# Single products for the attention's running maxima, a fourth bank for the scores, and context products in blocks of four key tiles

## The chip, the core and the metric

The kernel runs on one core of a Trainium2 chip. The metric is the time of one execution on the device in microseconds (us), taken as the median of several runs. All activations are float32. The kernel is written engine by engine: TensorE (matrix products), VectorE, ScalarE and GpSimd each have a program of their own, in a fixed order, and wait for one another on semaphores. TensorE writes its results to PSUM, which has eight banks of 512 float32 columns on 128 partitions.

## What is computed

A layer of latent attention, a mixture of experts, a second causal attention and a second mixture of experts, on x of 16 batches by 100 tokens by 256. The change touches only the first attention, which is, for each batch b:

```python
x = x + attention(layernorm(x), ctx_512)
# in attention, 16 heads, 1444 keys, latent width 64:
scores = einsum('bhsr,bhlr->bhsl', q_r, k_r)     # 16 x 100 queries against 1444 keys
attn   = softmax(scores, axis=-1)
ctx_c  = einsum('bhsl,bld->bhsd', attn, kv_r)    # context: 64 wide
out    = (ctx_c through w_kc_kv, heads joined) @ Wo.T
```

## The kernel before

`latent_attention` (L393) works batch by batch. The queries of a batch are 1600 columns (16 heads of 100), held as a high and a low part in `QS` (128 rows: 64 high, 64 low) and `QB`; the rotated keys lie in `KH` and `KB`, again with high and low parts. The 1444 keys are 12 tiles of 128, and the 16 heads are done in two passes p of 8 heads, so a batch has 24 tiles n, and a step m is two of them (n = 2m and 2m + 1).

For a tile, `scores` (L805) makes two half tiles (o = 0, 1) of 128 keys by 400 query columns, two matmuls each, into one of three banks (`SB`, `S0`). ScalarE takes the exponential of each half tile (L780) into `R`, a ring of eight tiles (`EB`). VectorE adds the even halves in a bank (`sum_even`, L599) and GpSimd the odd halves (`sum_odd`, L615); these are the softmax's divisors. `values` (L817) multiplies the exponentials with the rotated keys into the context (two half tiles, each on 64 columns of the array, beside each other).

The softmax subtracts each query's maximum, and it is found one batch ahead. Queries times keys, by the high parts, give 39 pieces (`NF`): 13 tiles of 128 queries by three overlapping ranges of 482 keys. `max_pair` (L555) makes two pieces at once on the two halves of the array's rows (64 rows each, the high parts of queries and keys) into two banks (`F0`), and `reduce_pair` (L585) on VectorE takes both maxima with one instruction over 964 columns. The next pair waits until that is done. After the twentieth, `batch_max` joins the three ranges, `turn_max` (L571) turns the result on TensorE, `max_high` and `max_low` split it, and two transfers of SyncE put it into rows of `QB`, where the scores' second matmul adds it.

In a step of TensorE (L828 on) stand: a pair of maxima of the next batch (for m below 10), the scores of two tiles, another pair, and the context products of the two tiles before. At step 2 come the column sums of the batch before (`sums`, second pass), at step 8 those of the first pass; at step 9 the output projection of the batch before (`project`, L662), at step 10 the turn. These share the bank `MISC`. VectorE's loop over n (L900) has the reduction of pair n, the running sum of tile n - 1, and at fixed n other work: the reciprocal of the divisors (`RECIP_AT`, n = 9), the division of the context (`CT_AT`, n = 14), two parts of the keys' low rows for the batch after next (`LO_AT`, n = 18 and 20, `rotate_part`, L540), the addition of the output (`add_output`) and `max_low`. GpSimd rotates the keys of the batch after next between its sums.

Of the kernel before, what the change touches and what calls it, by code (L numbers as in the profile page):

```python
# [12 lines left out]
ALU = mybir.AluOpType  # L13
# [7 lines left out]
P = 128  # L21
# [371 lines left out]
def latent_attention(core, dram, X, ident, queries, recips, BB):  # L393
# [14 lines left out]
    SB, FB = 3, 2  # L408
# [3 lines left out]
    S0, F0, CTX, ACC, MISC = 0, 3, 5, 6, 7  # L412
    SUM_AT, SUM0_AT, OUT_AT, TURN_AT = 2, 8, 9, 10
# [5 lines left out]
    with ExitStack() as ctx:  # L419
# [128 lines left out]
        def f_bank(b, i):  # L548

            return S0 if b is FIRST and i % 2 else F0  # L550
# [4 lines left out]
        def max_pair(pe, b, i):  # L555

            r = b_mod(b)
            depth = 2 if b is FIRST else 1
            if i >= depth:
                pe.wait_ge(red_done, b_val(b) * NP + (i - depth + 1))  # L560
            elif b is not FIRST:
                pe.wait_ge(red_done, b_val(b) * NP)
            for f in pieces(i):
                t, j = divmod(f, KC)
                rows = slice((f % 2) * DC, (f % 2 + 1) * DC)
                high = QB if f % 2 else QS
                last = nc.tensor.matmul(psum[f_bank(b, i) + f % 2][:, 0:KW], high[r][rows, t * P:(t + 1) * P],  # L567
                                        KH[r][rows, KAT[j]:KAT[j] + KW], start=True, stop=True)
            last.then_inc(f_ready, 1)

        def turn_max(pe, b):  # L571
            pe.wait_ge(nm_ready, b_val(b) + 1)
            nc.tensor.transpose(psum[MISC][0:QT, 0:P], NM[:, :], ident[:, :]).then_inc(turned, 1)

        def max_high(act, b):
            act.wait_ge(turned, b_val(b) + 1)
            if b is not FIRST:
                act.wait_ge(m_in, b_val(b) * 32)
            nc.scalar.activation(MH[:, :], psum[MISC][0:QT, 0:P], ACT.Copy).then_inc(mh_ready, 1)

        def max_low(v, b):
            v.wait_ge(mh_ready, b_val(b) + 1)
            nc.vector.tensor_tensor(ML[:, :], psum[MISC][0:QT, 0:P], as_f32(MH[:, :]), ALU.subtract).then_inc(ml_ready, 1)

        def reduce_pair(v, b, i):  # L585
            v.wait_ge(f_ready, b_val(b) * NP + (i + 1))
            if i == 0 and b is not FIRST:
                v.wait_ge(nm_ready, b_val(b))
            k, n = f_bank(b, i), len(pieces(i))
            nc.vector.tensor_reduce(PM[:, 2 * i:2 * i + n], banks[:, k:k + n, 0:KW], AX.X, ALU.max).then_inc(red_done, 1)  # L590

        def batch_max(v, b):
            v.wait_ge(red_done, b_val(b) * NP + NP)
# [36 lines left out]
        def sums(pe, b, p):  # L630
# [5 lines left out]
            for o in range(2):  # L636
                last = nc.tensor.matmul(psum[MISC][o * DC:(o + 1) * DC, 0:CH], ones[:], ES[:, p, o, :], start=True, stop=True)
            last.then_inc(sum_done, 1)

        def sums_out(act, b, p):  # L640
# [3 lines left out]
            nc.scalar.activation(SU[:, p, :], psum[MISC][0:DC + 1, 0:CH], ACT.Copy).then_inc(su_done, 1)  # L644
# [17 lines left out]
        def project(pe, b):  # L662

            pe.wait_ge(ct_ready, b_val(b) + 2)
            for j in range(H // 2):
                last = nc.tensor.matmul(psum[MISC][0:S, 0:D], CT[:, j, :], BB[:, j, :], start=j == 0, stop=j == H // 2 - 1)
            last.then_inc(out_ready, 1)

        def add_output(v, b):
            v.wait_ge(out_ready, b_val(b) + 2)  # L670
            x = X[:, b_val(b), :]
            nc.vector.tensor_tensor(x, psum[MISC][0:S, 0:D], x, ALU.add).then_inc(res_done, 1)
# [28 lines left out]
        with nc.Block() as block:  # L701
# [50 lines left out]
            def _(act):  # L752
# [13 lines left out]
                def step(b, has_next, has_keys):  # L766
                    for n in range(NS):
                        if n == 2 * TURN_AT + 2 and has_next:
                            max_high(act, b + 1)
                        if n == 0 and b is not FIRST:  # L770
                            context_out(act, before(b), 1)
                        act.wait_ge(av_done, b_val(b) * NS + (n + 1))
# [10 lines left out]
                        if n == 2 * SUM_AT + 1 and b is not FIRST:  # L783
                            sums_out(act, before(b), 1)
                        if n == KT + 1:
                            context_out(act, b, 0)
                        if n == 2 * SUM0_AT + 1:
                            sums_out(act, b, 0)
# [6 lines left out]
            def _(pe):  # L795
# [5 lines left out]
                for i in range(NP):  # L801
                    max_pair(pe, FIRST, i)
# [25 lines left out]
                def step(b, has_next, has_keys):  # L828
                    for m in range(NS // 2):
# [3 lines left out]
                        if has_next and 2 * m < NP:  # L833
                            max_pair(pe, b + 1, 2 * m)
                        if m == 0:
                            if b is not FIRST:
                                for n in range(NS - 2, NS):
                                    values(before(b), n)
                            if has_next:
                                max_pair(pe, b + 1, 1)  # L840
                            pe.wait_ge(m_in, b_val(b) * 32 + 32)
                        for n in (2 * m, 2 * m + 1):
                            scores(b, n)
                        if has_next and m and 2 * m + 1 < NP:
                            max_pair(pe, b + 1, 2 * m + 1)
                        if m == TURN_AT and has_next:
                            pe.wait_ge(su_done, b_val(b) * 2 + 1)
                            if b is not FIRST:
                                pe.wait_ge(res_done, b_val(b))
                            turn_max(pe, b + 1)  # L850
# [3 lines left out]
                        if m == SUM_AT and b is not FIRST:  # L854
                            sums(pe, before(b), 1)
                        if m == SUM0_AT:
                            sums(pe, b, 0)
                        if m == OUT_AT and b is not FIRST:
                            pe.wait_ge(su_done, b_val(b) * 2 + 1)
# [1564 lines left out]
```

## Time and profile before

| | us |
|---|---|
| median of three runs | 1990.33 |
| lowest and highest of them | 1978.36, 1990.39 |
| the profiled execution | 1987.93 |
| its span, first to last instruction | 1986.1 |

The profile is of one execution, and its rows are durations of instructions on each engine. Several in a row may be joined in a line with a count (x8 instructions). A matmul in float32 counts as two instructions. TensorE's matmuls overlap, so what a matmul costs is read from the start of one to the start of the next, and not from its duration; the same holds, for the last 0.1 us, on VectorE. What stands in brackets is the time for which the engine stood idle before the instruction, and who ended it. PE is TensorE, PEld its weight load, DVE VectorE, ACT ScalarE, POOL GpSimd; L567 is line 567. The attention's loop over batches runs from about 335 to 1190 us.

### The profile page before, as it was taken

The numbers are of one execution on the slowest core, as the hardware profiler recorded it, in microseconds if no ns is written. First come the engines' busy times: TensorE is split into PE (matmuls) and PEld (weight loads), VectorE is DVE, ScalarE is ACT, GpSimd is POOL, SyncE is SP. The second block draws the span as 40 slices with busy tenths as digits, with TensorE's granted clock in tenths as the row PEclk, the third lists the DMA queues.
The fourth block names the chain that finished last, engine by engine and source line by source line (L and its number), as shares of the span: only waits on it lengthen the run. The fifth ranks groups of instructions, "written<-read, shape, count | busy, mean of one in ns | idle before, by whom it ended". The sixth has DMA issues, their size and how long they took to land. (4 is left out here: it accounts for less than half of the span.)

```text
span 1986.1 us, 29082 instructions
## 1 busy us (share of the span) xinstructions
PE 1710.8 (86%) x9602; PEld 1155.4 (58%) x9602; DVE 1313.9 (66%) x2408; ACT 769.1 (39%) x1996; POOL 902.8 (45%) x800
## 2 busy tenths in 40 slices
PE   4999935999999999999999996499999559987890
PEld 3677712555555555555555553399999547664780
DVE  5577768777777777777777744377767666666333
ACT  2100001444444444444444442266656237652230
POOL 0366623777777777777777440223322100000436
PEclk9999965999999999999999996599999879988795
DMA  6133344122122221122221002545555250001243
GB/s 183 39 72 71 67 125 150 39 72 61 45 72 72 72 64 56 63 72 72 72 72 35 10 9 54 152 163 201 183 173 196 85 130 0 0 1 37 89 122 102
DMA packets 91670, 166.50 MB, mean 84 GB/s; under 512 B 45635, under 2 KB 70439, under 8 KB 86735
## 3 DMA queue, kind: packets, MB, share of 16 engines
q1 hardware_dynamic: 83727, 145.77, 23.8%
q0 software_dynamic: 7808, 19.02, 3.8%
q8 instruction: 73, 1.20, 0.3%
q14 instruction: 62, 0.51, 0.1%
HBM read 134.91 MB, written 29.53 MB: 83 GB/s over the span
## 5 line engine op out<-in xcount | busy, mean ns | idle before, releaser
L780 ACT ACTIVATE R<-banks 128x400 f32<-128x400 f32 x768 | 333.7, 505 | 342.4 <-PE banks L814 340.0
L590 DVE TENSOR_REDUCE PM<-banks 128x2 f32<-128x964 f32 x320 | 360.8, 1132 | 155.8 <-PE banks L567 154.1
L628 POOL TENSOR_TENSOR EA<-EA,R 128x400 f32<-128x400 f32 x288 | 313.3, 1088 | 177.8 <-ACT R L780 164.6
L814 PE MATMUL banks<-QS,KH 128*128 128x400 f32 x768 | 309.5, 403 | 3.0 <-DMA QB<-ML 2.1
L824 PE MATMUL banks<-R,KV 128*64 128x400 f32 x1536 | 299.9, 512 | 0.0
L814 PE MATMUL banks<-QB,KB 128*128 128x400 f32 x768 | 266.2, 347 | 0.0
L608 DVE TENSOR_TENSOR banks<-banks,R 128x400 f32<-128x400 f32 x320 | 183.9, 575 | 54.9 <-ACT R L780 54.2
L814 PEld LDWEIGHTS banks<-QS,KH 128*128 128x128 f32 x768 | 145.2, 189 | 109.0 <-ACT R L780 58.5
L567 PE MATMUL banks<-KH,QS 64*128 64x482 f32 x320 | 160.5, 502 | 53.5 <-DVE KB L540 46.3
L175 PE MATMUL banks<-e_xh,e_split 128*116 128x256 f32 x960 | 195.7, 287 | 4.0 <-DVE e_xl L1586 4.0
L380 POOL TENSOR_TENSOR rotated<-rope_prod 96x400 f32<-96x400 f32 x128 | 131.7, 1049 | 131.7 <-DVE rope_prod L357 131.6
L567 PEld LDWEIGHTS banks<-KH,QS 64*128 64x128 f32 x320 | 60.9, 191 | 197.2 <-issue 111.6
L824 PEld LDWEIGHTS banks<-R,KV 128*64 128x64 f32 x1536 | 93.4, 136 | 120.0 <-ACT R L780 67.1
L357 DVE TENSOR_TENSOR rope_prod<-banks,rope_q 96x400 f32<-96x400 f32 x256 | 128.6, 561 | 51.0 <-PE banks L175 51.0
L175 PEld LDWEIGHTS banks<-e_xh,e_split 128*116 128x116 f32 x960 | 153.1, 183 | 4.4 <-DVE e_xl L1586 4.4
L567 PE MATMUL banks<-KH,QB 64*128 64x482 f32 x304 | 153.0, 504 | 0.0
L814 PEld LDWEIGHTS banks<-QB,KB 128*128 128x128 f32 x768 | 146.5, 191 | 0.4
L1461 POOL DMA_INDIRECT results<-e_ys,m_target x40 | 44.4, 1109 | 213.1 <-DVE e_ys L1604 207.0
L175 PE MATMUL banks<-e_xl,e_split 128*116 128x256 f32 x480 | 136.7, 285 | 0.0
L521 POOL TENSOR_TENSOR raw<-raw,ropeT 128x722 f32<-128x722 f32 x60 | 104.0, 1735 | 53.8 <-DMA rawk<-in_ctx_k 53.8
L1052 POOL IOTA m_steps<- 100x7 f32 (+1 forms) x2 | 0.3, 158 | 237.8 <-POOLq L70 237.8
L1611 DVE TENSOR_TENSOR e_HF<-banks,e_G 116x256 f32<-116x256 f32 x120 | 50.5, 421 | 86.9 <-ACT e_G L1550 85.9
(281 smaller groups left out, 3368.9 us busy)
## 6 DMA issues: line engine op xcount, KB each, us to landing
m_stage_u<-in_m_up SPq DMA_DIRECT2D x20, 1392.0 KB
raw<-in_ctx_T SPq DMA_DIRECT2D x16, 1444.0 KB, 6.2
m_stage_d<-in_m_down SPq DMA_DIRECT2D x20, 696.0 KB
QS<-queries SPq DMA_DIRECT2D x16, 800.0 KB, 6.8
queries<-q_out_h SPq DMA_DIRECT2D x64, 100.0 KB, 2.4
queries<-q_out_l SPq DMA_DIRECT2D x64, 100.0 KB, 2.4
QB<-queries SPq DMA_DIRECT2D x16, 400.0 KB, 8.1
RS<-recips SPq DMA_DIRECT2D x32, 200.0 KB
```

What stands on the lines that cost most here:

```text
L175: ins = nc.tensor.matmul(out, lhs, rhs, start=first and n == 0, stop=last and n == len(todo) - 1)
L357: last = nc.vector.tensor_tensor(prod[:, h % 2, n, :].rearrange("p (b s) -> p b s", b=CB), psum[2 * (h % 2) + half][0:HALF, 0:CH].rearrang ...
L380: last = nc.gpsimd.tensor_tensor(rot[:, h % TURNS, half, :], prod[:, h % 2, 2 * half, :], prod[:, h % 2, 2 * half + 1, :], ALU.add)
L521: ins = ops.tensor_tensor(raw[:, row, half], raw[:, row, half], ropeT[:, row, half], ALU.mult)
L567: last = nc.tensor.matmul(psum[f_bank(b, i) + f % 2][:, 0:KW], high[r][rows, t * P:(t + 1) * P], KH[r][rows, KAT[j]:KAT[j] + KW], start=Tr ...
L590: nc.vector.tensor_reduce(PM[:, 2 * i:2 * i + n], banks[:, k:k + n, 0:KW], AX.X, ALU.max).then_inc(red_done, 1)
L608: ins = nc.vector.tensor_tensor(acc, acc, tile_of(n, 0), ALU.add)
L628: nc.gpsimd.tensor_tensor(out, first, tile_of(n, 1), ALU.add).then_inc(odd_sum, 1)
L780: nc.scalar.activation(tile_of(n, o), psum[S0 + (2 * n + o) % SB][:, 0:CH], ACT.Exp).then_inc(exp_done, 1)
L814: last = nc.tensor.matmul(out, lhs[r][:, keys], heads[:, o], start=lhs is KH, stop=lhs is KB)
L824: last = nc.tensor.matmul(psum[CTX][o * DC:(o + 1) * DC, 0:CH], KV[b_mod(b)][:, t, :], tile_of(n, o), start=t == 0, stop=t == KT - 1)
L1611: nc.vector.tensor_tensor(HF[:, b, :], psum[b][0:TR, TOK:2 * TOK], G[:, b, :], ALU.mult).then_inc(h_ready, 1)
```

## The change

The scores get four banks instead of three. The maxima get two banks, 4 and 5, that also serve the turn, the sums and the projection, which have no bank of their own any more. A piece of the maxima is now one matmul of all 128 rows (the high and the low part of the queries against the keys' high part), written to the two banks in turn, and reduced by an instruction of its own (`max_row`, `reduce_row`). The piece f waits until the piece f - 2 is reduced. A step has four slots for such pieces: ahead of the scores (0), between the two tiles' scores (1), behind them (2), and at the end of the step (3); the table `MAX_AT` says which are used. The context products stand in every second step, for four tiles, between slots 2 and 3 (in step 0: between slot 0 and the scores). Projection and output addition come a step later, behind the turn. The first batch's maxima, ahead of the loop, use four banks in pairs.

```diff
@@ constants @@
-    SB, FB = 3, 2
+    SB = 4
...
-    S0, F0, CTX, ACC, MISC = 0, 3, 5, 6, 7
-    SUM_AT, SUM0_AT, OUT_AT, TURN_AT = 2, 8, 9, 10
+    S0, F0, CTX, ACC = 0, 4, 6, 7
+    SUM_AT, SUM0_AT, TURN_AT = 2, 8, 10
+    MAX_AT = ((1, 1, 1, 1),) * 3 + ((0, 1, 1, 1),) + ((1, 1, 1, 1),) * 4 + ((1, 1, 1, 0), (0, 1, 1, 1), (1, 1, 0, 0), (0, 0, 0, 0))
+    MAX_NO = [[sum(map(sum, MAX_AT[:m])) + sum(MAX_AT[m][:slot]) for slot in range(4)] for m in range(NS // 2)]
+    MAX_SUM, MAX_SUM0 = MAX_NO[SUM_AT + 1][0], MAX_NO[SUM0_AT + 1][0]
...
+        def max_base(b):
+            return NP + (b_val(b) - 1) * NF if b is not FIRST else 0
...
-        def max_pair(pe, b, i):
...
+        def max_product(b, f, bank):
+            t, j = divmod(f, KC)
+            return nc.tensor.matmul(psum[bank][:, 0:KW], QS[b_mod(b)][:, t * P:(t + 1) * P],
+                                    KH[b_mod(b)][:, KAT[j]:KAT[j] + KW], start=True, stop=True)
...
+        def first_max(pe, i):
+
+            if i >= 2:
+                pe.wait_ge(red_done, i - 1)
             for f in pieces(i):
...
+                last = max_product(FIRST, f, S0 + 2 * (i % 2) + f % 2)
             last.then_inc(f_ready, 1)
...
+        def max_row(pe, b, f):
+
+
+            if f == 0:
+                pe.wait_ge(ml_ready, b_val(b))
+            elif f == 1:
+                if b_val(b) >= 3:
+                    pe.wait_ge(res_done, b_val(b) - 2)
+            else:
+                pe.wait_ge(red_done, max_base(b) + (f - 1))
+            if f == MAX_SUM and b_val(b) >= 2:
+                pe.wait_ge(su_done, 2 * b_val(b) - 2)
+            if f == MAX_SUM0:
+                pe.wait_ge(su_done, 2 * b_val(b) - 1)
+            max_product(b, f, F0 + f % 2).then_inc(f_ready, 1)
...
+        def reduce_row(v, b, f):
+            v.wait_ge(f_ready, max_base(b) + (f + 1))
+            if f == 0:
                 v.wait_ge(nm_ready, b_val(b))
...
+            nc.vector.tensor_reduce(PM[:, f:f + 1], psum[F0 + f % 2][:, 0:KW], AX.X, ALU.max).then_inc(red_done, 1)
...
@@ scalar @@
+                        if n == 2 * SUM_AT + 2 and b is not FIRST:
+                            sums_out(act, before(b), 1)
+                        if n == 2 * SUM0_AT + 2:
+                            sums_out(act, b, 0)
                         act.wait_ge(av_done, b_val(b) * NS + (n + 1))
...
@@ tensor @@
                 def step(b, has_next, has_keys):
+                    def max_slot(m, slot):
+                        if has_next and MAX_AT[m][slot]:
+                            max_row(pe, b + 1, MAX_NO[m][slot])
+
                     for m in range(NS // 2):
...
-                        if has_next and 2 * m < NP:
-                            max_pair(pe, b + 1, 2 * m)
+                        max_slot(m, 0)
                         if m == 0:
                             if b is not FIRST:
-                                for n in range(NS - 2, NS):
+                                for n in range(NS - 4, NS):
                                     values(before(b), n)
-                            if has_next:
-                                max_pair(pe, b + 1, 1)
                             pe.wait_ge(m_in, b_val(b) * 32 + 32)
-                        for n in (2 * m, 2 * m + 1):
-                            scores(b, n)
-                        if has_next and m and 2 * m + 1 < NP:
-                            max_pair(pe, b + 1, 2 * m + 1)
...
-                        for n in (2 * m - 2, 2 * m - 1):
-                            if n >= 0:
+                        scores(b, 2 * m)
+                        max_slot(m, 1)
+                        scores(b, 2 * m + 1)
+                        max_slot(m, 2)
+                        if m and m % 2 == 0:
+                            for n in range(2 * m - 4, 2 * m):
                                 values(b, n)
                         if m == SUM_AT and b is not FIRST:
+                            if has_next:
+                                pe.wait_ge(red_done, max_base(b + 1) + (MAX_SUM - 1))
...
                             sums(pe, before(b), 1)
                         if m == SUM0_AT:
...
                             sums(pe, b, 0)
...
+                        max_slot(m, 3)
+                        if m == TURN_AT:
+                            if has_next:
+                                turn_max(pe, b + 1)
+                            elif b is not FIRST:
+                                pe.wait_ge(res_done, b_val(b) - 1)
+                            if b is not FIRST:
+                                project(pe, before(b))
...
@@ vector @@
                     for n in range(NS):
-                        if has_next and n < NP:
-                            reduce_pair(v, b + 1, n)
+                        m, slot = n // 2, n % 2 * 2
+                        if has_next and MAX_AT[m][slot]:
+                            reduce_row(v, b + 1, MAX_NO[m][slot])
                         if n:
                             sum_even(v, b, n - 1)
                         elif b is not FIRST:
                             sum_even(v, before(b), NS - 1)
-                        if has_next and n == NP - 1:
+                        if has_next and MAX_AT[m][slot + 1]:
+                            reduce_row(v, b + 1, MAX_NO[m][slot + 1])
+                        if has_next and n == 2 * TURN_AT:
                             batch_max(v, b + 1)
...
-                        if n == 2 * OUT_AT + 2 and b is not FIRST:
-                            add_output(v, before(b))
                         if n == 2 * TURN_AT + 2 and has_next:
                             max_low(v, b + 1)
+                        if n == 2 * TURN_AT + 2 and b is not FIRST:
+                            add_output(v, before(b))
```

On TensorE in the middle of a batch, around the context products. The program names read: `banks<-KH,QS` at L567 (L560 after) is a piece of the maxima, `banks<-QS,KH` and `banks<-QB,KB` a half tile of scores, `banks<-R,KV` a half tile of context products; `at_red` is the semaphore of the reductions. Before:

```order
L814 MATMUL banks<-QS,KH 128x400 [waits at_exp]
L814 MATMUL banks<-QB,KB 128x400
L567 MATMUL banks<-KH,QS 128x482 [waits at_red]
L567 MATMUL banks<-KH,QB 128x482
L824 MATMUL banks<-R,KV 64x400 [waits at_exp]
L824 MATMUL banks<-R,KV 64x400
L824 MATMUL banks<-R,KV 64x400 [waits at_exp]
L824 MATMUL banks<-R,KV 64x400
L567 MATMUL banks<-KH,QS 128x482 [waits at_red]
L567 MATMUL banks<-KH,QB 128x482
L814 MATMUL banks<-QS,KH 128x400 [waits at_exp]
```

On TensorE in the changed kernel, the same place in an even step:

```order
L834 MATMUL banks<-QS,KH 128x400 [waits at_exp]
L834 MATMUL banks<-QB,KB 128x400
L560 MATMUL banks<-KH,QS 128x482 [waits at_red]
L844 MATMUL banks<-R,KV 64x400 [waits at_exp]
L844 MATMUL banks<-R,KV 64x400
L844 MATMUL banks<-R,KV 64x400 [waits at_exp]
L844 MATMUL banks<-R,KV 64x400
L844 MATMUL banks<-R,KV 64x400 [waits at_exp]
L844 MATMUL banks<-R,KV 64x400
L844 MATMUL banks<-R,KV 64x400 [waits at_exp]
L844 MATMUL banks<-R,KV 64x400
L560 MATMUL banks<-KH,QS 128x482 [waits at_red] x2
```

The block is twice as long; the two pieces behind it are slot 3 of the even step and slot 0 of the odd one.

On TensorE in the changed kernel, from an odd step to the next even one:

```order
L834 MATMUL banks<-QS,KH 128x400 [waits at_exp]
L834 MATMUL banks<-QB,KB 128x400
L834 MATMUL banks<-QS,KH 128x400 [waits at_exp]
L834 MATMUL banks<-QB,KB 128x400
L560 MATMUL banks<-KH,QS 128x482 [waits at_red] x3
L834 MATMUL banks<-QS,KH 128x400 [waits at_exp]
L834 MATMUL banks<-QB,KB 128x400
L834 MATMUL banks<-QS,KH 128x400 [waits at_exp]
L834 MATMUL banks<-QB,KB 128x400
L560 MATMUL banks<-KH,QS 128x482 [waits at_red]
```

With no context products in the odd step, three pieces stand one behind the other, each with a wait of its own.

On VectorE at the end of the maxima (n = 17 to 20). `PM<-banks` is a reduction, `banks<-banks,R` a running sum, `KB<-raw,KH` a part of the keys' low rows, `NM<-PM` the joining of the three ranges. Before:

```order
L590 TENSOR_REDUCE PM<-banks 128x2 [waits at_f]
L608 TENSOR_TENSOR banks<-banks,R 128x400 [waits at_evensum,at_exp]
L540 TENSOR_TENSOR KB<-raw,KH 64x722 [waits at_kh,at_rotstep]
L590 TENSOR_REDUCE PM<-banks 128x1 [waits at_f]
L608 TENSOR_TENSOR banks<-banks,R 128x400 [waits at_evensum,at_exp]
L596 TENSOR_REDUCE NM<-PM 128x13 [waits at_turned,at_red]
```

On VectorE in the changed kernel, the same place:

```order
L628 TENSOR_TENSOR banks<-banks,R 128x400 [waits at_evensum,at_exp] x2
L610 TENSOR_REDUCE PM<-banks 128x1 [waits at_f]
L544 TENSOR_TENSOR KB<-raw,KH 64x722 [waits at_kh,at_rotstep]
L610 TENSOR_REDUCE PM<-banks 128x1 [waits at_f]
L628 TENSOR_TENSOR banks<-banks,R 128x400 [waits at_evensum,at_exp]
L610 TENSOR_REDUCE PM<-banks 128x1 [waits at_f] x2
L628 TENSOR_TENSOR banks<-banks,R 128x400 [waits at_evensum,at_exp]
L610 TENSOR_REDUCE PM<-banks 128x1 [waits at_f]
L616 TENSOR_REDUCE NM<-PM 128x13 [waits at_turned,at_red]
```

Behind the keys' part stood one reduction and now stand four, over two steps.

## Rows read from the trace of the kernel before

**Rows 1.** The page's first line.

```profile
span 1986.1 us, 29082 instructions
```

**Rows 2.** TensorE's timeline at two turns; the window between (busy by engine, clock, DMA).

```profile
601.49 0.27 PE L573 MATMUL banks<-ident,NM 128*13 128x128 f32 x1
...
655.13 0.27 PE L573 MATMUL banks<-ident,NM 128*13 128x128 f32 x1
...
601.49:655.13 53.64, 53.64 (x257) 28.84 (x256) 39.77 (x52) 24.26 (x56) 39.13 (x33) 1.00 0.22 67
```

**Rows 3.** Waits of that window: total us, times, longest us.

```profile
DVE PM L590 <- PE banks L567: 10.0, 16, 2.0
...
PEld banks L567 <- DVE PM L590: 4.4, 7, 0.6
```

**Rows 4.** Timeline of TensorE, one step (m = 4): start us, us, what.

```profile
624.03 0.48 PE L567 MATMUL banks<-KH,QS 64*128 64x482 f32 x1
...
624.45 0.45 PE L814 MATMUL banks<-QS,KH 128*128 128x400 f32 x1
624.74 0.35 PE L814 MATMUL banks<-QB,KB 128*128 128x400 f32 x1
...
625.48 0.34 PE L814 MATMUL banks<-QB,KB 128*128 128x400 f32 x1
625.76 0.45 PE L814 MATMUL banks<-QS,KH 128*128 128x400 f32 x1
626.05 0.35 PE L814 MATMUL banks<-QB,KB 128*128 128x400 f32 x1
626.33 0.48 PE L567 MATMUL banks<-KH,QS 64*128 64x482 f32 x1
...
626.74 1.56 PE L824 MATMUL banks<-R,KV 128*64 128x400 f32 x8
628.24 0.48 PE L567 MATMUL banks<-KH,QS 64*128 64x482 f32 x1
```

**Rows 5.** The same timeline: the projection, and four tiles in a row.

```profile
649.92 3.70 PE L666 MATMUL banks<-BB,CT 128*100 128x256 f32 x16
653.27 0.54 PE L814 MATMUL banks<-QS,KH 128*128 128x400 f32 x1
...
1141.28 0.34 PE L814 MATMUL banks<-QB,KB 128*128 128x400 f32 x1
1141.55 2.91 PE L824 MATMUL banks<-R,KV 128*64 128x400 f32 x16
1144.39 0.45 PE L814 MATMUL banks<-QS,KH 128*128 128x400 f32 x1
```

**Rows 6.** A single product and its reduction; VectorE's other work in a batch (busy, mean ns).

```profile
1130.87 0.48 PE L567 MATMUL banks<-KH,QS 64*128 64x482 f32 x1
...
1131.39 0.66 DVE L590 TENSOR_REDUCE PM<-banks 128x1 f32<-128x482 f32 x1 [0.62 <-PE banks L567]
1131.96 0.57 DVE L608 TENSOR_TENSOR banks<-banks,R 128x400 f32<-128x400 f32 x1
1132.45 0.18 DVE L596 TENSOR_REDUCE NM<-PM 128x13 f32<-128x39 f32 x1
...
L540 DVE TENSOR_TENSOR KB<-raw,KH 64x722 fp32r<-64x722 f32 x2 | 2.7, 1327 | 0.1
...
L659 DVE TENSOR_TENSOR CT<-CU,RS 128x800 f32<-128x800 f32 x1 | 1.0, 981 | 0.0
L653 DVE RECIPROCAL RR<-SR 16x100 f32<-16x100 f32 x1 | 0.8, 755 | 0.0
```

**Rows 7.** TensorE in batch 1: a wait for the rows of maxima, and the window behind.

```profile
393.31 0.45 PE L814 MATMUL banks<-QS,KH 128*128 128x400 f32 x1 [2.12 <-DMA QB<-ML]
...
398.59 0.48 PE L567 MATMUL banks<-KH,QS 64*128 64x482 f32 x1
...
394.00:397.50 3.50, 3.50 (x12) 2.48 (x11) 1.64 (x2) 1.94 (x5) 1.04 (x1) 0.51 0.00 0
```

More of the change, by code:

```diff
@@ L411, in latent_attention @@
     PAD = -1.0e30
-    S0, F0, CTX, ACC, MISC = 0, 3, 5, 6, 7
-    SUM_AT, SUM0_AT, OUT_AT, TURN_AT = 2, 8, 9, 10
+    S0, F0, CTX, ACC = 0, 4, 6, 7
[3 more added lines that the diff above has]
+    MAX_SUM, MAX_SUM0 = MAX_NO[SUM_AT + 1][0], MAX_NO[SUM0_AT + 1][0]
+    assert sum(map(sum, MAX_AT)) == NF and MAX_SUM % 2 == 0 and MAX_SUM0 % 2 == 0
     RECIP_AT, CT_AT = 9, 14
@@ L636, in sums @@
             for o in range(2):
-                last = nc.tensor.matmul(psum[MISC][o * DC:(o + 1) * DC, 0:CH], ones[:], ES[:, p, o, :], start=True, stop=True)
+                last = nc.tensor.matmul(psum[F0][o * DC:(o + 1) * DC, 0:CH], ones[:], ES[:, p, o, :], start=True, stop=True)
             last.then_inc(sum_done, 1)
@@ L643, in sums_out @@
                 act.wait_ge(sr_in, b_val(b) * 32)
[L644 removed]
+            nc.scalar.activation(SU[:, p, :], psum[F0][0:DC + 1, 0:CH], ACT.Copy).then_inc(su_done, 1)
         def context_out(act, b, p):
@@ L665, in project @@
             for j in range(H // 2):
-                last = nc.tensor.matmul(psum[MISC][0:S, 0:D], CT[:, j, :], BB[:, j, :], start=j == 0, stop=j == H // 2 - 1)
+                last = nc.tensor.matmul(psum[F0 + 1][0:S, 0:D], CT[:, j, :], BB[:, j, :], start=j == 0, stop=j == H // 2 - 1)
             last.then_inc(out_ready, 1)
@@ L671, in add_output @@
             x = X[:, b_val(b), :]
-            nc.vector.tensor_tensor(x, psum[MISC][0:S, 0:D], x, ALU.add).then_inc(res_done, 1)
+            nc.vector.tensor_tensor(x, psum[F0 + 1][0:S, 0:D], x, ALU.add).then_inc(res_done, 1)
         class Batch:
@@ L855, in step @@
                             sums(pe, before(b), 1)
                         if m == SUM0_AT:
+                            if has_next:
+                                pe.wait_ge(red_done, max_base(b + 1) + (MAX_SUM0 - 1))
                             sums(pe, b, 0)
-                        if m == OUT_AT and b is not FIRST:
-                            pe.wait_ge(su_done, b_val(b) * 2 + 1)
-                            project(pe, before(b))
+                        max_slot(m, 3)
+                        if m == TURN_AT:
+                            if has_next:
+                                turn_max(pe, b + 1)
[3 more added lines that the diff above has]
+                                project(pe, before(b))
@@ L862, in _ @@
                 steps(pe, step)
-                for n in range(NS - 2, NS):
+                for n in range(NS - 4, NS):
                     values(LAST, n)
+                pe.wait_ge(su_done, 2 * B - 1)
+                sums(pe, LAST, 1)
                 pe.wait_ge(res_done, B - 1)
-                sums(pe, LAST, 1)
-                pe.wait_ge(su_done, 2 * B)
                 project(pe, LAST)
```

45 lines of the change are left out of this document (12 added, 33 removed).

## Prediction

> **What bounds the kernel now.** I read the page first: one core, a span of 1986.1 us [rows 1]. The latent attention is a loop over 16 batches, and from the turn of one batch's maxima to the next turn it takes 655.13 - 601.49 = 53.64 us; in that window TensorE is busy without a gap at the full clock, VectorE for 39.77 us, ScalarE for 24.26, GpSimd for 39.13 [rows 2]. The reader should see that TensorE alone is full. The waits of the same window say it from the other side: VectorE waited 10.0 us for the products of the maxima, while the products waited only 4.4 us for VectorE's reductions [rows 3]. So VectorE has slack, but it is slack scattered between the steps.
>
> Then the timeline of TensorE in one step of two key tiles [rows 4]: pair of products at 624.03, eight score matmuls from 624.45, second pair at 626.33, two tiles of context products at 626.74, next step at 628.24. A step is 4.21 us: 0.42 for the first pair, 1.88 for the scores, 0.41 for the second pair, 1.50 for the context products. Score matmuls follow at 0.184 us (624.74 to 625.48 is four of them); the first one after another form of matmul, or after a wait for a bank, is followed 0.29 us later. Four tiles in a row stand in the last batch: 1141.55 to 1144.39, 2.84 us, entered 0.27 us after the last score matmul [rows 5].
>
> **The change on TensorE.** Two steps now hold 16 score matmuls, eight single products and one block of four tiles. No row shows a product over 128 rows and 482 columns. From below it is 0.184 us (the spacing of a score matmul of 400 columns), from above 0.29 (a weight load not hidden); I take 0.184 x 482/400 = 0.22, since it sits among score matmuls of the same form. Sum: 16 x 0.184 + 0.11 (first after the block) + 8 x 0.22 + 2.84 + 0.09 (entry) = 7.74 us against 2 x 4.21 = 8.42. The fourth score bank is in it: the 0.29 waits at each step's last half tile go, at 0.10 each for two spacings. If nothing else waited, five such pairs of steps would save 5 x 0.68 = 3.4 us a batch, and the pair of steps without products (4.21 - 0.83 = 3.38 a step before; the sum without products, 5.98, now) 0.8 more.
>
> **The change on VectorE.** It now has 39 reductions of 482 columns for 19 of 964 and one of 482. A single one is seen at 1131.39: it lasts 0.66, the next instruction starts 0.57 later, the running sum after it holds 0.49, and it started 0.52 after its product (1130.87) [rows 6]. Eight reductions and four sums in two steps are 8 x 0.57 + 4 x 0.49 = 6.5 us, less than 7.7; by load alone it would fit.
>
> But it does not fit in time. There are only two banks, so product f waits for the reduction of product f-2. One product stands behind the block of context products, and the seven others of the two steps ahead of the next block. Walk it from the start of a block at 0. VectorE finishes what it has at about 1.4 and then has nothing: the next product comes at 2.84. Its reduction runs 3.36 to 4.02. Then, without a gap: reduction of slot 0 at 3.93, running sum at 4.50, slot 1 at 4.99 (ends 5.65), slot 2 at 5.56 (ends 6.22), running sum 6.13, slot 3 at 6.62 (ends 7.28). TensorE meanwhile: slot 0 at 3.17, scores, slot 1 at 4.13, scores, slot 2 at 5.08; slot 3 would come at 5.30 but waits until 5.65; slot 0 of the next step would follow and waits until 6.22; scores 6.55 to 7.28; slot 1 at 7.28, just as its bank comes free; scores to 8.25; slot 2 and the entry, and the next block starts at 8.56. So a pair of steps costs 8.6, not 7.7: 0.2 more than before. The 2 us in which VectorE stood idle beside the block are lost.
>
> Bounds of this walk: if a reduction holds VectorE for its whole 0.66, four of them on the chain add 0.36 a pair of steps; if the products take 0.184 or 0.29, the three behind the last wait move it by -0.1 to +0.2. I keep 0.57, seen where an instruction was ready behind one.
>
> Now the places where the walk is not the plain one, from block to block over a batch:
> - m = 0 to 2: here the block stands ahead of the scores, so eight products in steps 0 and 1 and three in step 2 run with no block between. The same walk gives 11.4.
> - m = 2 to 4: two more pairs of column matmuls for the sums (0.67, by the spacing 2.84/8) delay slot 3, but step 3 has a product less: 9.0.
> - m = 4 to 6: the reciprocal (0.755 busy, some 0.67 net) [rows 6] stands right behind the reduction of slot 3, at the start of the chain: 8.6 + 0.7 = 9.3. Before, it lay in VectorE's slack.
> - m = 6 to 8: the division (0.981, some 0.9 net) stands between slots 1 and 2 of step 7: 9.5.
> - m = 8 to 10: the subtraction of the keys' high part (mean 1.327) [rows 6] stands between the first and the second reduction of step 9. TensorE reaches slot 0 of step 10 at about 5.7 and gets the bank at 7.3. To the block: 9.7, where the sums are in it. Before, the projection (649.92 to 653.27, 3.35 us) [rows 5] stood here and covered this subtraction; it now comes two steps later, behind all products, so the cover is gone.
> - m = 10 to the next batch: block 2.84, turn 0.27, projection 3.35, eight score matmuls 1.58, product and entry 0.31: 8.4.
> Sum 57.3 against 53.64: +3.66 us a batch.
>
> The turn now stands ahead of the projection; behind it come 3.35 + 1.58 + 0.31 + 2.84 = 8 us of TensorE's work before the scores that need the rows of maxima, so no wait appears. The output add on VectorE holds its queue until the projection ends; behind it stand only a running sum and the first reduction of the next batch, which has 1 us left. ScalarE and GpSimd keep their work, and eight buffers still cover blocks of four.
>
> **The clock.** TensorE stood still for 2.12 us ahead of 393.31, for the rows of maxima, and the stretch from 394.0 to 397.5 was granted 0.51, the lower level of 1.2 GHz [rows 7]. Scores, a pair and the next scores took 398.59 - 393.31 = 5.28 us instead of 1.88 + 0.42 + 1.88 = 4.18, so it cost 1.1. My longest stall, 1.6 us at step 10's first product, is shorter. Between 0 and 1.1 a batch I take 0.3.
>
> A rule of the Trainium skill speaks against this change: "TensorE: Matmul & The Clock Gate", section "A second HAM failure mode: psum-queue depth-cycling", says that a kernel which cycled PSUM banks idled briefly between groups of matmuls often enough that its clock swung between the two levels. The stretch at 0.51 agrees in kind; no row here shows it for stalls under half a microsecond.
>
> **Sum.** Batches 1 to 14: 14 x 3.66 = 51. Batch 0 has products but no reciprocal and division: 3.66 - 1.6 = +2. The last has no products: six pairs of steps at -0.8 = -4.8. Clock: 14 x 0.3 = 4. Together +52. The profiled execution took 1987.93 us (span 1986.1 and 1.8 around it), 2.4 under the median of 1990.33: 1987.9 + 52 = 2040 us. The first batch's own maxima keep four banks and are paced by VectorE as before: nothing.
>
> **Rivals.**
> A, faster: VectorE keeps up behind the block, and the sum of TensorE counts. Per batch -3.4 - 0.8 = -4.2, fifteen times, and -4.8: -68, 1920 us. For it: VectorE's 39.77 busy of 53.64 and its 6.5 of 7.7 above. Against it: the order of products and reductions is fixed on both engines, and the idle stretch beside the block can't be used with one product behind it. It would need the chain from 3.36 to 7.28 to be 0.8 shorter.
> B, no change: waits about half of what I walked, as a few of the running sums or reductions are shorter than the rows say: 1970 to 2010, say 1990.
> C, slower still, by the clock: not one stall a batch but several let it fall. At 1.1 each, six a batch in fifteen batches: +99 in place of the 4, 2135 us. For it: [rows 7], and the page's rule above by its kind. Against it: in the walk TensorE works 7.7 of 8.6 us.
>
> **How the numbers follow.** My forecast 0.74, A 0.12, B 0.07, C 0.07. Less than 1% either way is about what a measurement of this kernel can't tell from no change; so faster 0.12, same 0.07, slower 0.74 + 0.07 = 0.81. Bounds of the forecast: products at their low end take 0.5 a batch off and a subtraction of half its mean 0.7, 17 us in all, and I leave as much again for what the walk has put on the chain wrongly, 2005; the 0.66 reductions add 1.8 a batch (27 us) and dips of the clock at 1.1 instead of 0.3 another 11: 2080 (rounded up). That range leaves out A, most of C and part of B, some 2 in 10.
>
> **What would show it.** Right: turn to turn 57 to 58 us; the products' line waiting for VectorE some 10 us a batch instead of 4.4; VectorE idle for about 2 us beside each block of four tiles; no waits of score matmuls for ScalarE inside a step; the longest wait at the first product of step 10. Wrong: a period under 53 us with VectorE waiting for products throughout; products spaced over 0.3 us with nothing waiting; or a granted clock well below 1.00 over the whole loop (C).

## The result, and the profile after

The changed kernel takes 2044.64 us (median of four runs, 2043.76 to 2045.09) against 1988.63 us for the one before. The measured ratio is 1.0299, with a 95% interval of 1.0267 to 1.0331 (the two medians alone give 1.0282). It is slower by 56 us; 2040 was forecast. The span of its profiled execution is 2043.3 us, 57.2 more than [rows 1]. Medians here and below are of a kernel's fast runs: one run of f1, one of f2 and two of g1 took at least 4% longer than their others and are left out.

First TensorE's timeline at two turns and the window between, which answer to [rows 2]:

```profile
619.69 0.28 PE L589 MATMUL banks<-ident,NM 128*13 128x128 f32 x1
...
677.72 0.28 PE L589 MATMUL banks<-ident,NM 128*13 128x128 f32 x1
...
619.69:677.72 58.03, 52.91 (x258) 33.05 (x257) 40.34 (x71) 25.03 (x55) 39.77 (x32) 1.00 0.19 62
```

From turn to turn, which is called a batch below, it takes 58.03 us instead of 53.64. TensorE was busy throughout; now it is for 52.91 and stands for 5.1. The granted clock is 1.00. The waits of that window, against [rows 3]:

```profile
DVE PM L610 <- PE banks L560: 13.2, 7, 2.8
PEld banks L560 <- DVE PM L610: 9.8, 18, 2.1
...
PE banks L560 <- DVE PM L610: 4.9, 7, 1.8
```

The weight loads of the products (PEld) wait for VectorE 9.8 us instead of 4.4, and the matmuls themselves, which stood for none of the window in [rows 2], 4.9. VectorE waits for products more as well (13.2 instead of 10.0): each engine stands while the other has work that can't come yet. Where, TensorE's timeline shows, from the block at step 6 to the one at step 10 (block starts at 654.83, 664.75, 674.88):

```profile
654.83 2.91 PE L844 MATMUL banks<-R,KV 128*64 128x400 f32 x16
...
657.67 0.70 PE L560 MATMUL banks<-KH,QS 128*128 128x482 f32 x2
...
662.34 0.49 PE L560 MATMUL banks<-KH,QS 128*128 128x482 f32 x1 [1.33 <-DVE PM L610]
...
664.75 2.91 PE L844 MATMUL banks<-R,KV 128*64 128x400 f32 x16
...
672.57 0.49 PE L560 MATMUL banks<-KH,QS 128*128 128x482 f32 x1 [1.85 <-DVE PM L610]
...
674.88 2.91 PE L844 MATMUL banks<-R,KV 128*64 128x400 f32 x16
```

and VectorE over the same stretch:

```profile
658.19 1.22 DVE L610 TENSOR_REDUCE PM<-banks 128x1 f32<-128x482 f32 x2 [2.11 <-PE banks L560]
659.33 0.57 DVE L628 TENSOR_TENSOR banks<-banks,R 128x400 f32<-128x400 f32 x1
659.81 0.65 DVE L610 TENSOR_REDUCE PM<-banks 128x1 f32<-128x482 f32 x1
660.38 1.33 DVE L679 TENSOR_TENSOR CT<-CU,RS 128x800 f32<-128x800 f32 x1
661.63 0.65 DVE L610 TENSOR_REDUCE PM<-banks 128x1 f32<-128x482 f32 x1
...
669.52 0.66 DVE L610 TENSOR_REDUCE PM<-banks 128x1 f32<-128x482 f32 x1 [2.83 <-PE banks L560]
670.21 1.61 DVE L544 TENSOR_TENSOR KB<-raw,KH 64x722 fp32r<-64x722 f32 x1
671.85 0.66 DVE L610 TENSOR_REDUCE PM<-banks 128x1 f32<-128x482 f32 x1
```

VectorE is idle for 2.11 and 2.83 us beside the blocks; behind each idle stretch stands its other work (division, keys' part), and behind that the reduction for which TensorE then waits 1.33 and 1.85 us.

### The profile page after: what moved, and what is told of

It is laid out like the page before. It is cut to its first block and busy times, and to the rows that moved or that the text cites. A ratio compares the mean times of both kernels' runs of the same rounds, so it can differ in the third digit from the quotient of the medians.

```text
span 2043.3 us, 29381 instructions
## 1 busy us (share of the span) xinstructions
PE 1696.5 (83%) x9602; PEld 1222.8 (60%) x9602; DVE 1321.3 (65%) x2693; ACT 779.0 (38%) x1996; POOL 910.4 (45%) x800
## 5 line engine op out<-in xcount | busy, mean ns | idle before, releaser
L610 DVE TENSOR_REDUCE PM<-banks 128x1 f32<-128x482 f32 x585 | 363.7, 648 | 202.0 <-PE banks L560 200.0
L804 ACT ACTIVATE R<-banks 128x400 f32<-128x400 f32 x768 | 341.8, 505 | 310.8 <-PE banks L834 294.5
L560 PE MATMUL banks<-KH,QS 128*128 128x482 f32 x624 | 269.5, 458 | 121.7 <-DVE PM L610 70.9
L844 PE MATMUL banks<-R,KV 128*64 128x400 f32 x1536 | 279.1, 505 | 0.0
L834 PE MATMUL banks<-QS,KH 128*128 128x400 f32 x768 | 273.5, 356 | 1.5 <-DMA QB<-ML 1.5
L560 PEld LDWEIGHTS banks<-KH,QS 128*128 128x128 f32 x624 | 117.9, 196 | 240.4 <-DVE PM L610 144.7
L844 PEld LDWEIGHTS banks<-R,KV 128*64 128x64 f32 x1536 | 101.7, 136 | 138.9 <-issue 124.6
L2209 ACT ACTIVATE c_PR<-banks,c_nmax 100x100 f32<-100x100 f32 x256 | 83.9, 355 | 48.3 <-DVE c_nmax L2253 48.3
```

The costliest lines, as they stand in the source:

```text
L560: return nc.tensor.matmul(psum[bank][:, 0:KW], QS[b_mod(b)][:, t * P:(t + 1) * P], KH[b_mod(b)][:, KAT[j]:KAT[j] + KW], start=True, stop=True)
L610: nc.vector.tensor_reduce(PM[:, f:f + 1], psum[F0 + f % 2][:, 0:KW], AX.X, ALU.max).then_inc(red_done, 1)
L804: nc.scalar.activation(tile_of(n, o), psum[S0 + (2 * n + o) % SB][:, 0:CH], ACT.Exp).then_inc(exp_done, 1)
L834: last = nc.tensor.matmul(out, lhs[r][:, keys], heads[:, o], start=lhs is KH, stop=lhs is KB)
L844: last = nc.tensor.matmul(psum[CTX][o * DC:(o + 1) * DC, 0:CH], KV[b_mod(b)][:, t, :], tile_of(n, o), start=t == 0, stop=t == KT - 1)
L2209: nc.scalar.activation(PR[u][:, h, :], psum[SC + 2 * u + h // HB][0:S, (h % HB) * S:(h % HB + 1) * S], ACT.Exp, bias=nmax[u][:, 1, h:h + 1 ...
```

## The experiments

**First round: what costs the 4.4 us a batch?** Theory: blocks of four tiles, with one product behind them and two banks, put VectorE's work on a chain. Rival: the single products and their 39 reductions cost it. e1 undoes the blocks alone; in e2 the kernel before gets the blocks alone. "Turn" in the expectations is the time from turn to turn. Behind each median stands its ratio to the kernel before, measured again beside it, and the 95% interval of that ratio.

```diff
 # e1, on the changed kernel; e2 does the reverse to the kernel before
-for n in range(NS - 4, NS):
+for n in range(NS - 2, NS):
...
-if m and m % 2 == 0:
-    for n in range(2 * m - 4, 2 * m):
+if m:
+    for n in range(2 * m - 2, 2 * m):
```

> The changed kernel with its context products put back into every step, two tiles at a time; everything else stays changed (single products, four score banks, two banks for the maxima, projection behind the turn). My theory (a block of four leaves VectorE idle and then makes eight reductions run through two banks in a burst) expects no burst: a step of 4.05 us by TensorE's own sum, the two products behind one block reduced well before they are needed; turn to turn about 52 us against 57.98 after and 53.64 before, 1966 us. Rival 1 (the single products and their 39 reductions are what costs, whatever the blocks) expects the time to stay near 2040. Rival 2 (the clock) expects nothing, as the changed kernel's loop shows 1.00.

> The kernel before with one edit: context products for four tiles in every second step. Pairs of products, reductions over 964 columns, three score banks as before. My theory expects the burst here too: behind the block the first pair of the odd step, the second pair, and the first pair of the next step, each waiting for the reduction of the pair before; 9.5 us for two plain steps against 8.42, turn to turn 58 us, 2058 us in all. Rival 1 (single products cost, blocks are free or better) expects a gain: one entry into the block less in two steps, some 0.2 us, so 53 us turn to turn and 1970 to 1985.

e2 took 2063.47 us (1.0379, 1.0339 to 1.042), with turns 58.15 apart in most batches: blocks of four cost the kernel before 4.5 us a batch too, with its pairs. In the first three intervals and two later ones it was 60.7 to 61.3, and each of these was granted a lower clock: 0.76 in the first, 0.94 in the others (one of them is 748.05 to 808.78, 60.73 us).

e1 took 2029.05 us (1.0212, 1.0175 to 1.0248), far above the 1966 expected. Its batches, from the third on, come in two kinds: three took 54.1 us and nine 58.0 to 58.5 (the last, 53.2, has no keys' part). In a long batch VectorE's timeline and GpSimd's show this, and TensorE's what follows:

```profile
824.17 4.36 DVE L679 TENSOR_TENSOR CT<-CU,RS 128x800 f32<-128x800 f32 x1
```

```profile
823.86 1.07 POOL L648 TENSOR_TENSOR EA<-EA,R 128x400 f32<-128x400 f32 x1
824.86 1.83 POOL L539 TENSOR_TENSOR KV<-rawk,prodk 128x768 f32<-128x768 f32 x1
826.64 1.04 POOL L648 TENSOR_TENSOR EA<-EA,R 128x400 f32<-128x400 f32 x1
```

```profile
829.15 0.49 PE L560 MATMUL banks<-KH,QS 128*128 128x482 f32 x1 [3.11 <-DVE PM L610]
...
784.93:843.27 58.34, 54.53 (x259) 33.88 (x257) 43.88 (x71) 25.27 (x55) 38.98 (x33) 0.97 0.19 61
```

The division ends 0.85 us after GpSimd's third instruction in a row, and alone it takes 0.98: it seems to have waited for all three. TensorE stands for 3.11 us, and the stretch behind is granted the lower clock. In a short batch the division (at 770.04) took 1.59 us and the KV instruction, at 770.70, 2.61: there GpSimd waited. So e1's total doesn't price single products; a new question came of it, taken up in the second round.

e3 keeps the blocks of four and moves VectorE's other work beside them: the reciprocal and the division (n = 13) ahead of the reduction of slot 3, the keys' parts to n = 17 and 20. e4 lets the loop's reductions read 241 of the 482 columns (it leaves out half of each maximum's range).

```diff
 # e3
-RECIP_AT, CT_AT = 9, 14
-HI_AT, LO_AT = (17, 18), (18, 20)
+RECIP_AT, CT_AT = 9, 13
+HI_AT, LO_AT = (16, 18), (17, 20)
...
+if n == RECIP_AT and b is not FIRST:
+    reciprocals(v, before(b))
+if n == CT_AT and b is not FIRST:
+    divide(v, before(b))
 if has_next and MAX_AT[m][slot + 1]:
...
 # e4
-psum[F0 + f % 2][:, 0:KW]
+psum[F0 + f % 2][:, 0:KW // 2]
```

> The changed kernel with VectorE's other work moved into its idle time beside the blocks of four: the reciprocal ahead of the reduction of slot 3 of step 4, the division there in step 6 (n = 13), the first subtraction of the keys' high part to n = 17, right at the block of step 8 (ScalarE's part of it a tile earlier). Nothing else. My theory expects each to leave the chain: step 4 to 6 from 9.29 to 8.6, 6 to 8 from 9.92 to 8.6, 8 to 10 from 10.13 to about 8.3; turn to turn 54.1 instead of 57.98, so some -55 us, 1990 us. If the slots behind the block are not the chain, it changes under 10 us.

> The changed kernel with each reduction in the loop reading 241 of the 482 columns (half of each piece is left out of the maximum); all products, waits and their order stay. A reduction then costs VectorE 0.32 instead of 0.57. My theory (VectorE's chain sets the time) expects the plain pair of steps to fall from 8.56 to about 8.2 (three products in a row still wait for a reduction each), the reciprocal hidden, and turn to turn 54 us, 1985 us. If TensorE's own work or the banks' switching sets the time, nothing changes: 2044.

e3: 1995.63 us (1.0046, 1.0025 to 1.0067), e4: 1969.67 (0.9916, 0.9888 to 0.9945). Their windows, then e4's reductions in one:

```profile
656.79:711.45 54.66, 52.56 (x258) 33.03 (x256) 40.02 (x71) 24.92 (x55) 39.97 (x32) 1.00 0.20 65
...
596.75:649.94 53.19, 50.85 (x258) 33.49 (x256) 31.00 (x71) 25.04 (x55) 40.14 (x32) 1.00 0.23 68
```

```profile
L610 DVE TENSOR_REDUCE PM<-banks 128x1 f32<-128x241 f32 x39 | 15.1, 402 | 17.9 <-PE banks L560 17.7
```

The same instructions in another place give e3 back 3.4 of the 4.4 us a batch, and VectorE is hardly less busy (40.02 for 40.34); the keys' part is 0.5 us shorter there, the division 0.2 longer. With reductions of 0.40 us instead of 0.65 e4's period is 53.2. e3 says that the chain through VectorE sets the time, not VectorE's load and not the product's price on TensorE. e4 agrees, but it lightens the load as well as the chain.

**Second round: is e1's long division GpSimd's doing, and what else has a price?** f1 is e1 with the division at n = 16. f2 is e1 with e3's order on VectorE (division at n = 15). f3 is f2 with three score banks, f4 is f2 with the first batch's maxima as pairs.

```diff
 # f1, on e1
-RECIP_AT, CT_AT = 9, 14
+RECIP_AT, CT_AT = 9, 16
 # f3, on f2
-SB = 4
+SB = 3
 # f4, on f2, in first_max
+rows = slice((f % 2) * DC, (f % 2 + 1) * DC)
+last = nc.tensor.matmul(psum[S0 + 2 * (i % 2) + f % 2][:, 0:KW], (QB if f % 2 else QS)[0][rows, ...
```

> The single products with the context products in every step (e1), and nothing else changed but that the division stands at n = 16 and no longer at n = 14, where GpSimd had three instructions back to back. Theory (the 4.36 us division beside those three made e1's slow batches): the division takes 0.98 to 1.6 us in every batch, all turns are 54.1 us apart at a clock of 1.00, and the time is e3's 1996 - 15 x 0.5 = 1988. Rival (single products with so little behind a step's end let the clock fall by themselves, wherever the division is): batches of 58 stay, 2015 to 2030.

> Single products, context products in every step, and the reciprocal (n = 9) and the division (n = 15) ahead of the reduction of slot 3, so that they lie beside the context products; the keys' parts at n = 17 and 20. Theory (VectorE's other work was on the chain of products and reductions, and the time beside the context products is free): TensorE's own sum, 10 steps of 4.1, two of 3.1, sums 0.67, projection 3.35, turn 0.3 = 51.5, with some 1 us of waits left: turns 52.5 apart, 1996 - 15 x 2.1 = 1964. Rival (with two tiles the 1.5 us beside the block are too short for it, VectorE has no slack there): 54.1 as e1's good batches, 1988.

> f2 with three banks for the scores instead of four. Theory (the fourth bank takes away the spacing of 0.29 instead of 0.184 at each step's last half tile): two such spacings of 0.1 a step in 12 steps, +2.4 us a batch, f2 + 37 us. Rival (a single product between the two tiles' scores gives ScalarE the time that the bank gave): same as f2 within 8 us.

> f2, and the first batch's maxima ahead of the loop as 64-row pairs on the two halves of the array, as the kernel before has them, in the changed kernel's four banks. Theory (the prologue's loss of 3.4 us is the two products one behind the other instead of side by side): the turn of the first batch 3 us earlier, f2 - 3 us. Rival (VectorE sets the pace there whatever TensorE does): no difference to f2, within 1 us.

f1: 1977.89 us (0.9953, 0.9924 to 0.9982), division 1.3 to 1.8 us, turns 53.4 apart at 1.00 in most batches: one number moved, and e1's 58 us batches are gone. f2: 2004.38 (1.0074, 1.0047 to 1.0101), not the 1964 expected. Its division fell on GpSimd's KV instruction again; VectorE's row of a long batch and of the one batch where it went well, then GpSimd's of the same times:

```profile
699.85 3.58 DVE L679 TENSOR_TENSOR CT<-CU,RS 128x800 f32<-128x800 f32 x1
...
867.68 1.07 DVE L679 TENSOR_TENSOR CT<-CU,RS 128x800 f32<-128x800 f32 x1
```

```profile
699.75 1.84 POOL L539 TENSOR_TENSOR KV<-rawk,prodk 128x768 f32<-128x768 f32 x1
701.54 2.77 POOL L648 TENSOR_TENSOR EA<-EA,R 128x400 f32<-128x400 f32 x2
...
867.84 2.61 POOL L539 TENSOR_TENSOR KV<-rawk,prodk 128x768 f32<-128x768 f32 x1
```

KV 0.10 us earlier than the division: 3.58, and a turn of 56.74. KV 0.16 us later: 1.07, and that batch's turn is 52.70. In eleven other batches KV came 0.10 to 0.15 us earlier; the division took 2.6 us, with turns of 54.2, or 3.5 to 3.6. Of the batches with 3.5 to 3.6 two kept a clock of 1.00 and took 55.2, and five were granted 0.97 and took 56.4 to 57.5; one of each:

```profile
659.85:716.59 56.74, 53.81 (x258) 33.51 (x256) 42.35 (x71) 25.14 (x55) 39.23 (x33) 0.97 0.21 63
937.26:992.47 55.21, 52.29 (x259) 32.55 (x257) 42.46 (x71) 25.05 (x55) 39.23 (x33) 1.00 0.21 65
```

So the waiting division costs 1.5 us a batch at 2.6 and 2.5 at 3.5 to 3.6, and the lower clock, where it comes, about 1.6 more.

f3: 2014.36 (1.0148, 1.0127 to 1.0169), 10 over f2, but its divisions were mostly 3.5 to 3.6 against f2's 2.6 to 3.6. Its one undisturbed batch (division 1.02) took 52.87 against f2's 52.70, and its batches with 3.5 at a clock of 1.00 took 55.4 against f2's 55.2: in this order, with a single product between the two tiles' scores, the fourth score bank is worth 0.2 us a batch, and the expected 37 us fell. f4: 2001.85 (1.0077, 1.0057 to 1.0098), whose total can't be told from f2's; the rows at its start can. f4 makes a pair every 1.07 us, f2 two pairs in 2.43, both at a granted clock of 0.50:

```profile
312.92 0.76 PE L570 MATMUL banks<-KH,QS 64*128 64x482 f32 x1 [0.30 <-DVE PM L607]
...
313.98 0.77 PE L570 MATMUL banks<-KH,QS 64*128 64x482 f32 x1 [0.30 <-DVE PM L607]
```

```profile
311.49 2.24 PE L560 MATMUL banks<-KH,QS 128*128 128x482 f32 x4 [0.46 <-DVE PM L604]
313.92 2.24 PE L560 MATMUL banks<-KH,QS 128*128 128x482 f32 x4 [0.19 <-DVE PM L604]
```

f4's first turn is at 331.88, f2's at 334.12. Counted from the first product (309.82 and 309.09) that is 22.06 us against 25.03, the 3 us expected; the start itself moves by 2.5 us from kernel to kernel.

**Third round: from GpSimd's side.** g2 leaves VectorE as in f2 and moves only GpSimd's KV. g1 leaves GpSimd and moves VectorE's work to where it had stood idle. g3 is g2 with f4's start.

```diff
 # g2, on f2
-ROT_AT = (3, 4, 5, 6, 8, 9, 10, 11, 13, 14)
+ROT_AT = (3, 4, 5, 6, 8, 9, 10, 11, 13, 16)
 # g1, on f4; the first part at n = 19 also stands ahead of slot 3
-RECIP_AT, CT_AT = 9, 15
-HI_AT, LO_AT = (16, 18), (17, 20)
+RECIP_AT, CT_AT = 9, 17
+HI_AT, LO_AT = (17, 18), (19, 20)
```

> f4 with the division at n = 17 and the first part of the keys at n = 19 ahead of slot 3, where GpSimd stood idle in f2's and f1's traces. Theory (f2 and f4 were slow only because the division at n = 15 began within 0.1 us of GpSimd's KV instruction and lost to two or three instructions in a row, 2.6 to 3.6 us; the one batch of f2 with a division of 1.07 had a turn of 52.70): the division takes 1.0 to 1.1 in every batch, all turns 52.7 apart at a clock of 1.00, f1's 1979.7 - 15 x 0.7 - 2 (first batch as in f4) = 1967. Rival (the order with work beside the block is itself worse than f1's): turns of 53.4 or more, 1978 or more.

> f2 with nothing changed on VectorE, TensorE and ScalarE; only GpSimd's last key instruction (KV) comes at n = 16 instead of n = 14. Theory (the division's length is set by what GpSimd has to run beside it): at n = 15 it meets one sum at most, 1.0 to 2.1 us, turns of 52.7 to 54.2 with no dip of the clock, 1970 to 1990. Rival (the division waits for something of its own, its operands RS and CU or the projection before): 2.6 to 3.6 us and turns of 54.2 to 56.9 as in f2, 2005.

> g2 with the first batch's maxima as 64-row pairs, as in f4. Theory: turns of 52.7 apart as in g2, and the first turn 2 us earlier, as f4's 331.9 against f2's 334.1: 1968 - 2 = 1966. Rival (the first turn depends more on when the first loads land than on the products): as g2, 1968, within its 4 us.

g2: 1968.02 us (0.9896, 0.9865 to 0.9927); a division and a window of it:

```profile
637.99 0.98 DVE L679 TENSOR_TENSOR CT<-CU,RS 128x800 f32<-128x800 f32 x1
```

```profile
597.98:650.69 52.71, 52.22 (x259) 32.57 (x257) 40.28 (x71) 24.93 (x55) 39.51 (x33) 1.00 0.22 68
```

The division takes 0.98 in nearly every batch and ten of its turns are 52.7 apart: with VectorE's program unchanged, GpSimd's order alone took 36 us off f2. g1 (1979.03; 0.9951, 0.9931 to 0.9971) missed, and its rival's numbers came out: most turns are 53.5 to 54.0 apart, two are 54.5 and 55.4, with waits of 0.86 and 3.86 us for the rows of maxima. In about half of its batches the division met the last of three sums of GpSimd (1.83), but that isn't what the turns show: the turn is 53.50 and 53.53 in two batches with 1.83 and 0.98. In both, and in every batch that has a keys' part, TensorE stands for 0.74 to 0.76 us at a product whose bank is reduced behind that part; the rows of the one with 1.83:

```profile
916.00 1.64 DVE L544 TENSOR_TENSOR KB<-raw,KH 64x722 fp32r<-64x722 f32 x1
```

```profile
918.39 0.49 PE L560 MATMUL banks<-KH,QS 128*128 128x482 f32 x1 [0.76 <-DVE PM L613]
```

In the last batch of the loop, which has none, it doesn't stand there, and the turn is 52.6. So what stood on the chain was the keys' part at n = 19. g3: 1966.29 (0.9903, 0.9874 to 0.9932), turns of 52.7, first turn at 331.91; its total can't be told from g2's. Both are some 1% faster than the kernel before, with intervals below 1, and faster than the changed one.

## Why the prediction was right

The forecast was right in sign and size by its own mechanism, the chain of two banks behind a long block: slower, 57.2 us of span for the 52 reckoned. That the sum came so near is in part luck, for terms that were too small and one that was too large offset each other.

- **The walk from block to block.** Read between the starts of the blocks from 616.85 to 674.88, forecast first: m = 10 to the next batch 8.4 and 8.18; 0 to 2, 11.4 and 11.43; 2 to 4, 9.0 and 9.08; 4 to 6, 9.3 and 9.29; 6 to 8, 9.5 and 9.92; 8 to 10, 9.7 and 10.13. The plain pair of steps, reckoned at 8.6, stands free of other work in e3: 8.67. A single product among scores is followed 0.22 later (628.70 to 628.92), as worked out from columns. The column sums, put at 0.67, took 0.77 (639.20 to 639.97); two of the spacings of 2.84/8 named for them are 0.71.
- **Two terms mis-sized.** The division took 1.33 for 0.981: it was charged as on VectorE alone, but it shares with GpSimd, as f1 and g2 show. The keys' subtraction took 1.61 for 1.327, and 1.327 was the mean of two unlike parts. The one that now stands on the chain is the first, and in the kernel before the two were:

```profile
647.93 1.75 DVE L540 TENSOR_TENSOR KB<-raw,KH 64x722 fp32r<-64x722 f32 x1
...
651.70 0.91 DVE L540 TENSOR_TENSOR KB<-raw,KH 64x722 fp32r<-64x722 f32 x1
```

  With both corrected the walk gives 57.9 for the 58.0 measured. A batch costs 4.4 and not 3.66: 12 batches, +52 instead of +44.
- **The clock** was charged 4 us, 0.3 in each of 14 batches. It fell in one, batch 1, behind a stall of 1.34 us:

```profile
428.91 0.49 PE L560 MATMUL banks<-KH,QS 128*128 128x482 f32 x1 [1.34 <-DVE PM L610]
...
432.76 2.91 PE L844 MATMUL banks<-R,KV 128*64 128x400 f32 x16
...
430.00:432.00 2.00, 2.00 (x8) 1.92 (x7) 1.62 (x3) 1.08 (x3) 1.60 (x2) 0.50 0.00 0
```

  From that product to the block it took 3.85 us, where a later batch took 2.41 (662.34 to 664.75): the dip cost 1.4. The batches behind it were granted 1.00 in spite of the same stalls of 1.33 and 1.85 us. Rival C, several dips in every batch, didn't come about; e1, f2 and e2 have one or two in some of their batches. The rule of the Trainium skill that was weighed ("TensorE: Matmul & The Clock Gate", section "A second HAM failure mode: psum-queue depth-cycling") speaks of brief and frequent stops. e2, with four stalls of 1.25 to 1.43 us a batch, agrees with it in kind, though ten of its fifteen batches kept 1.00; in e1 and f2 the clock fell behind one stall of 2.4 to 3.4 us a batch, which is another case, and in the changed kernel it fell in the one batch.
- **Batch 1** grew by 0.65 only (57.54 for 56.89). Behind its first turn, at 388.19, the next matmul is one of the scores (388.22): the projection now comes behind the turn, and the first one falls into the next batch. So this batch has lost 3.3 us of projection (619.80 to 623.07 in a later one) to the stretch behind the last turn, which now holds three and not two. The wait for the rows of maxima came all the same, 1.50 us for the 2.12 of [rows 7].
- **The prologue** was charged nothing and cost 3.4 us (first turn at 335.14, before 331.72). The step that failed: "paced by VectorE as before". The two products of a pair ran side by side on the halves of the array and now run one behind the other, at a granted clock of 0.50, and VectorE waits for the second. From the first product to the first turn it takes 25.04 us (from 310.10) for 22.06 (from 309.66); f4, with pairs, takes 22.06 again. The other 0.4 is the later start.
- **The rest.** Batch 0: +1.0 for +2. The batch before the last: +2.6 for +3.66; the keys' part, which is in the 3.66, doesn't occur in it. From the last turn on: -2.9 for -4.8, with one projection more in it. Together with 52, 0.65 and 3.4 this makes up the 57.2, but for rounding.
- **Rival A** (TensorE's sum counts) priced a batch at 49.4. Even with half-length reductions e4's took 53.2, in which TensorE was busy for 50.85 and stood for 2.3: the chain still held it up, as argued against A, and TensorE's own sum was above A's too. What it saw rightly, that single products cost TensorE less, comes out with two tiles: steps of 4.09 to 4.12 in g2 for 4.21.

The periods of undisturbed batches, side by side: pairs with two tiles 53.64, pairs with four 58.15, single products with four 58.0, with two 54.13 (e1), 53.4 (f1) and 52.7 (g2). So with VectorE's other work where it was, the blocks cost about 4 us a batch with either kind of products (4.5 with pairs, 3.9 with single ones against e1). With that work moved beside the block they cost half of it: 54.6 in e3 against 52.7 in g2, whose division is also 0.6 shorter. The single products, with the fourth bank and VectorE's other work beside the blocks, save up to 0.9 a batch with two tiles. Not tried: a third bank for the maxima behind blocks of four.

## What to carry to other kernels

Slack that is summed over a loop says nothing on whether work fits; walk the chain of products, banks and reductions from one long block to the next, and put the other work of the slack engine beside the block and not behind it. Before a VectorE instruction with two operands in SBUF is moved, look at what GpSimd runs at that moment, for tenths of a microsecond there decided between 52.7 and 56.9 us a batch in f2, the lower clock included.

## What was not expected of the hardware

The division's length goes from 0.98 to 4.65 us by where it falls against GpSimd's instructions, while reductions (0.65) and running sums (0.57) keep theirs beside the same work. The Trainium skill, page "SBUF — State Buffer", section "Who interferes with whom", says that a VectorE instruction with two inputs in SBUF contends with a GpSimd instruction that reads SBUF, that the shared ports are an exclusive lock, and that the order of issue decides who blocks; the rows agree where two instructions meet (GpSimd's KV 2.61 for 1.83 where the division was first). With three they don't follow the order of issue: the waiting division can lose again to one that begins after it. In e1 it began 0.31 us into a sum, and two more instructions went ahead of it (4.36); in the short batch it began 0.34 us into one (769.70) and was next (1.59). What decides that stays open.

Of the clock: within one kernel the same stall of TensorE was followed by the lower level (0.50) in one batch and not in another. In the changed kernel a stall of 1.34 us was in batch 1, and 1.32 to 1.35 and 1.83 to 1.85 were not in the batches behind it. In f2 five stalls of 2.39 to 2.48 us were, and two of 2.44 and 2.45 (ahead of 981.48 and 1090.95) were not. In e1 all of the ten stalls of 3.10 to 3.40 us were. In e2 stalls of 1.26 and 1.43 us stand in batches granted 0.94 and in batches granted 1.00 alike. What decides is not settled.
